# Weighting of the gathered expert rows moved between the first-layer banks of the recurrence's network; its last quarter finished in two halves

## The reference

```python
# s: a phase recurrence and a small network
context = jnp.concatenate([cm_real, cm_imag, ret_real, ret_imag], axis=-1)   # [B, S, 4*128]
h = _layernorm(context, ln_gamma, ln_beta)
h = jax.nn.gelu(jnp.einsum('bsd,ed->bse', h, W1) + b1, approximate=False)    # 256 wide: first layer
h = jnp.einsum('bsd,ed->bse', h, W2) + b2                                    # 128 wide: second layer
s = x + h
# g: experts with a capacity; each token's two gates weight the two rows it gets back
out = jnp.einsum('EGCM,GSEC->GSM', expert_outputs, combine)
x = x + s * silu(out)
```

## Time and profile before

| | |
|---|---|
| median of 3 runs | 681.86 us (681.68 to 682.83) |
| profiled execution, kernel time | 679.72 us |
| its span, first to last instruction | 677.8 us |
| TensorE busy | 598.5 us, 88% |
| VectorE busy | 483.6 us, 71% |
| ScalarE busy | 329.5 us, 49% |
| mean granted TensorE clock | 0.949 of full speed |

### The profile page before, as it was taken

One profiled execution on the slowest core, in us unless ns is written; L12 is line 12 of the kernel. 1 busy time (PEld: TensorE's weight loads), 2 busy tenths in 40 slices (PEclk: granted clock), 3 DMA queues, 4 the chain that ended last, 5 costly groups with the idle time before them and its releaser, 6 DMA issues.

```text
span 677.8 us, 12462 instructions
## 1 busy us (share of the span) xinstructions
PE 598.5 (88%) x4233; PEld 368.6 (54%) x4260; DVE 483.6 (71%) x1184; ACT 329.5 (49%) x586; POOL 159.6 (24%) x146
## 2 busy tenths in 40 slices
PE   2878999999999998999999958844999799999995
PEld 1524543534444446999999524342346356656553
DVE  7799989999888986555555882067998399832437
ACT  1742566665757666555555577520233352352322
POOL 2000000000233330333333100000078668722200
PEclk9877999999999999999999998966899799999997
DMA  8970606051631621111110510260012133310401
GB/s 187 253 268 3 226 2 196 17 181 45 173 96 33 167 83 38 48 49 50 47 47 25 154 43 1 57 195 0 0 43 64 21 104 107 99 37 16 120 20 62
DMA packets 53676, 57.18 MB, mean 84 GB/s; under 512 B 8635, under 2 KB 37339, under 8 KB 53579
## 3 DMA queue, kind: packets, MB, share of 16 engines
q1 hardware_dynamic: 49294, 49.73, 26.2%
q0 software_dynamic: 4320, 6.81, 3.1%
q10 hardware_dynamic: 12, 0.01, 0.0%
HBM read 42.19 MB, written 18.85 MB: 90 GB/s over the span
## 4 chain that ended last, share of the span: by engine, by line
PE 61%; DVE 26%; issue 5%; ACT 4%; DMA 1%; SPq 1%; another core or an unknown queue 0%; DVEq 0%; ACTq 0%
PE banks L1479 10%; PE banks L1600 7%; PE banks L1725 6%; PE banks L1541 6%; PE banks L1491 5%; PE banks L1558 5%; DVE arena L1071 5%; PE banks L1714 4%; DVE mpart L1074 4%; PE banks L1711 4%; PE banks L1770 3%; DVE mpart L1069 2%; ACT arena L693 2%; PE banks L1544 2%; PE banks L1423 1%
## 5 line engine op out<-in xcount | busy, mean ns | idle before, releaser
L693 ACT ACTIVATE arena<-banks 128x512 f32<-128x512 f32 (+1 forms) x304 | 156.1, 586 | 98.0 <-PE banks L1544 55.9
L1558 PE MATMUL banks<-arena 96*128 96x512 bf16 (+3 forms) x384 | 120.4, 344 | 6.6 <-DVE mpart L1071 2.0
L1541 PE MATMUL banks<-arena 128*128 128x512 bf16 (+3 forms) x358 | 106.7, 327 | 12.6 <-ACT arena L693 9.0
L1074 DVE TENSOR_REDUCE mpart<-banks 128x1 f32<-128x512 f32 x128 | 85.9, 684 | 9.5 <-PE banks L1558 9.0
L1071 DVE CUSTOM_DVE_ANT_0 arena<-banks,arena 128x512 bf16<-128x512 f32 (+1 forms) x128 | 76.7, 617 | 9.7 <-PE banks L1558 6.5
L1479 PE MATMUL banks<-arena 128*128 128x128 f32 x624 | 76.3, 275 | 1.0 <-ACT arena L643 1.0
L1479 PEld LDWEIGHTS banks<-arena 128*128 128x128 f32 x624 | 72.8, 192 | 1.5 <-ACT arena L643 1.5
L1600 PE MATMUL banks<-arena 128*9 128x512 f32 (+3 forms) x768 | 71.4, 491 | 0.0
L1541 PEld LDWEIGHTS banks<-arena 128*128 128x128 bf16 x384 | 37.6, 99 | 60.5 <-issue 27.3
L739 ACT ACTIVATE arena<-banks 125x512 f32<-125x512 f32 (+2 forms) x48 | 28.6, 596 | 78.7 <-PE banks L1711 55.3
L544 POOL DMA_INDIRECT slots<-rows_a,posn x16 | 15.5, 969 | 192.9 <-PE banks L1541 179.4
(11 more groups left out here) (268 smaller groups left out, 904.3 us busy)
## 6 DMA issues: line engine op xcount, KB each, us to landing
k_parts<-arena SPq DMA_DIRECT2D x6, 768.0 KB, 7.9
arena<-in_L_ffn_experts_w_dram SPq DMA_DIRECT2D x2, 2048.0 KB, 10.7
arena<-results SPq DMA_DIRECT2D x8, 512.0 KB, 6.8
arena<-k_parts SPq DMA_DIRECT2D x7, 576.0 KB
arena<-q_parts SPq DMA_DIRECT2D x28, 144.0 KB
arena<-in_L_ffn_w_kernel_dram SPq DMA_DIRECT2D x8, 344.0 KB
slots<-in_pad_rows_dram SPq DMA_DIRECT2D x1, 2535.0 KB, 11.8
arena<-slots SPq DMA_DIRECT2D x39, 65.0 KB
```

The costliest lines, as they stand in the source:

```text
L693: act.activation(Pr[:, r % 4, heads[0]:heads[-1] + 1, 0:n], ring_e[e % 3][:, 0:len(heads) * n].rearrange("p (j c) -> p j c", j=len(heads)) ...
L1074: ins = dve.tensor_reduce(part, ps[:, 0:n], AX_X, ALU.max)
L1541: ins = pe.matmul(ring_e[e % 3][:, at * n:at * n + n], QK[:, slot, j, 1, P * kt:P * kt + P], QK[:, slot, j, 0, q:q + n], start=True, stop= ...
L1558: ins = pe.matmul(ps[:, at * n:at * n + n], QK[0:TALL, slot, j, 0, P * i:P * i + P], QK[0:TALL, slot, j, 1, 512 * half:512 * half + n], st ...
```

## The change

VectorE's order is written anew: `weighted(0)` stands behind scaled(3), `weighted(1)` behind scaled(4), `finish(1, 0)` and `finish(1, 1)` behind scaled(6), and `finish(1, 2)` behind attended(2). The last quarter is finished by a new function, `last_half(i)`, in two halves of two tiles: three instructions of 256 columns each. For that, `layer_2(3)` puts its tiles 2 and 3 into the other bank of `psM`, signals after two tiles and again after four, and waits between them for attended(2), which reads that bank. SyncE stores the last quarter in two transfers.

```diff
-            for c in range(4):
-                sp.wait_ge(Z["x2_done"], c + 1)
-                sp.dma_start(out_t[:, 4 * c:4 * c + 4, :], x1[:, 4 * c:4 * c + 4, :]).then_inc(Z["out_done"], 16)
-            sp.wait_ge(Z["out_done"], 64)
+            for i, (t0, t1) in enumerate(((0, 4), (4, 8), (8, 12), (12, 14), (14, 16))):
+                sp.wait_ge(Z["x2_done"], i + 1)
+                sp.dma_start(out_t[:, t0:t1, :], x1[:, t0:t1, :]).then_inc(Z["out_done"], 16)
+            sp.wait_ge(Z["out_done"], 16 * 5)
...
-            for c in range(4):
-                scaled(2 * c)
-                scaled(2 * c + 1)
-                if c:
-                    attended(c - 1)
-                if c == 2:
-                    weighted(0)
-                    weighted(1)
-            for c in range(3):
+            def last_half(i):
+
+                tiles = slice(12 + 2 * i, 14 + 2 * i)
+                dve.wait_ge(Z["h2_ps"], 4 + i)
+                link(dve.tensor_tensor(s_sb[:, tiles, :], psM[:, 1 - i, 256 * i:256 * i + 256].rearrange("p (n d) -> p n d", d=D),
+                                       s_sb[:, tiles, :], ALU.add))
+                link(dve.tensor_tensor(ya[:, tiles, :], ya[:, tiles, :], s_sb[:, tiles, :], ALU.mult))
+                dve.tensor_tensor(x1[:, tiles, :], x1[:, tiles, :], ya[:, tiles, :], ALU.add).then_inc(Z["x2_done"], 1)
+
+            for u in range(4):
+                scaled(u)
+            weighted(0)
+            attended(0)
+            scaled(4)
+            weighted(1)
+            scaled(5)
+            attended(1)
+            scaled(6)
+            for c in range(2):
                 finish(1, c).then_inc(Z["x2_done"], 1)
-            attended(3)
-            finish(1, 3).then_inc(Z["x2_done"], 1)
+            scaled(7)
+            attended(2)
+            finish(1, 2).then_inc(Z["x2_done"], 1)
+            for i in range(2):
+                last_half(i)
...
-                        ins = pe.matmul(psM[:, c % 2, P * n:P * n + P], h1g[:, o, q:q + P], W2T_sb[:, o, :], start=(o == 0), stop=(o == 1))
-                ins.then_inc(Z["h2_ps"], 1)
+                        ins = pe.matmul(psM[:, (c + (c == 3 and n >= 2)) % 2, P * n:P * n + P], h1g[:, o, q:q + P], W2T_sb[:, o, :], start=(o == 0), stop=(o == 1))
+                    if n == 3 or (c, n) == (3, 1):
+                        ins.then_inc(Z["h2_ps"], 1)
+                    if (c, n) == (3, 1):
+                        pe.wait_ge(Z["s1_done"], 3)
```

## The result

| | before | after |
|---|---|---|
| median | 682.13 us (681.68 to 682.83, 5 runs) | 678.54 us (677.77 to 679.24, 5 runs) |
| ratio | | 0.9951, 95% interval 0.9938 to 0.9963 |
| profiled execution | 679.72 us, span 677.8 | 678.54 us, span 676.6 |

The change makes the kernel faster by 3.59 us between the medians, 2.5 to 4.2 by the interval. The forecast was 677.7, in a range from 676.2 to 679.8, with 0.93 on faster.

A forecast was written before the change was run, and what follows sets the result against it. Work on VectorE and ScalarE unrelated to the matmuls was taken to hold 11 us of the end; moved weighting and halves end VectorE at 671.35, plus 2.3 store: span 673.65, 4.15 less, median 677.7 us, range 676.2 to 679.8.

The forecast's parts named there:

- signs of being wrong: TensorE idle ahead of the last bank, DMA-ended idle ahead of line 1381, or the first 647 us changed.
- The moved weighting: VectorE: weighted(0) fits behind scaled(3), 4.25 us of work in 4.6; weighted(1) behind scaled(4) delays scaled(5) by 0.85 us.
- The closing of TensorE's hole: TensorE ahead of layer_2(3): it starts at 666.66 without a hole, 3.0 us earlier than before.
- The halves: VectorE's last quarter: six instructions at 0.416 us, ending at 671.35; the halving pays its own cost and no more.
- The store: Output's end: the span ends 2.3 us behind VectorE's last instruction instead of 2.77; bounds 2.77 and 2.27.
- The table loads: ScalarE around the two Silus: 1.28 us for each load, with the Gelu table back at 663.3.
- rival 1: ScalarE or TensorE still holds the end; TensorE idles again and returns at half clock: 679.1 us, chance 0.09.
- The thin spare: Ahead of layer_2(3): the Gelu of u=7 ends at 666.4, 0.3 us before layer_2(2) ends at 666.66.
- Rival 3: VectorE: weighted(0) waits for the expert rows in front of scaled(4); slower, 684 if they land at 656; chance 0.03.
- free up to 1.3 us: Rival 3's late expert rows: no cost up to some 1.3 us (Silu 660.9 against use at 662.2), then one for one.
- break-even at 5.5: Rival 3's expert rows: lateness decides against the change when they land 5.5 us after 648.3, at 653.8.

The follow-up runs named there:

- the weights first: SyncE issues expert 4's loads ahead of its wait for the scattered destinations: 669.66 us in the changed kernel, 673.95 us in the kernel before.
- the filler: Changed kernel with three or six chained multiplications of 128x1024 on a dead region ahead of weighted(0): 679.65 us with three, 683.92 us with six.

## Why the prediction was right

**The start of the stage.** One of my signs of being wrong did come: the first 647 us are not those of before, for scaled(3) starts at 650.60. It says nothing against the working from there on. The runs with the weights first, the old order and the new, start it at 641.93 and 642.10, so nothing shows that the change moves anything ahead of it, and 2.4 of the 3.0 us are the difference between two holes upstream.

**The moved weighting.** Right in place and size. With the 3.0 us of later start taken off, weighted(1) ends into a scaled(5) at 657.0 (said: 657.1), the first Silu starts at 659.8 (said: 659.8), the Gelu table is back at 663.1 (said: 663.3), scaled(7) starts at 664.9 (said: 664.95), VectorE ends at 671.34 (said: 671.35). Every term was a duration of a row and every start the later of two rows.

**What gains.** I put the gain to the moved weighting. The number came out because the sum had the finishes in their new place; the sentence named the wrong part. The weighting moved by itself is worth 0.2 to 0.3 us; it is the finishes of the first two quarters ahead of the end of layer_2(2) that shorten the end, by 2.6 us, and the weighting had to move only so far that the first Silu is done when finish(1, 0) could start. One weighting was enough for that. The closing of TensorE's hole, which I counted among the steps, gains little without the finishes. Finishes ahead with neither weighting moved was not run: they would wait for the Silus.

**The halves.** Right: 26.00 us to the end of the span with and without them. The six instructions took 0.42 to 0.43 us each, the nearest row had 0.416. The Trainium skill's figure (VectorE: DVE Perf Modes, the section on the TRN2 errata) of 424 ns, an estimate from the page's formula, agrees, and so does its warning: the halving buys nothing here in the new order.

**The store.** Right: 2.26 against 2.3, half of the transfer's 1.0 us.

**The table loads.** The Trainium skill (ScalarE: Activation LUTs, What ACT_TABLE_LOAD costs) counts 2.66 us for each change of tables, a load of 1283 ns and about 1380 ns to drain. The trace has the load at 664.79, 1.28 long, and the Gelu at 666.08, so the measurement has no such drain. As an estimate from the page's figure, two changes at 2.66 would have brought the Gelu of u=7 to its end near 670.2, and TensorE a hole of 0.5 us ahead of layer_2(3); there is none. In rival 1 I had said that a Gelu followed at once on both loads; in the rows it did on the second only, and the Silu behind the first waited 3.41 us for VectorE. In the profile after, both are followed at once.

**The thin spare and rival 1.** The Gelu of u=7 ended at 669.35, layer_2(2) at 669.67: 0.3 us, as said. That it lay so close did no harm, and would have done none: with only the first weighting moved, TensorE idles 0.40 us there, and the stage is the same. Nor did it return at half clock, as rival 1 has it: behind holes of 0.40, 0.77 and 1.70 us the last group took 2.05 us each time, at a clock of 1.00.

**Rival 3's terms.** Mis-sized. I put lateness as free up to 1.3 us and break-even at 5.5. In the changed kernel VectorE idles 0.46, 0.34, 2.80 and 1.09 us behind scaled(3), 4.69 in all (three of them in the rows shown, the 0.34 ahead of attended(1)), and every one of these can take up lateness; I had counted the slack of the first Silu alone. With the filler what is left idle is 1.83 us (three), ahead of the first finish, and 0.82 and 1.04 (six), ahead of scaled(6) and the first finish. So 2.86 and 2.83 us are taken up, and the rest is paid: 0.89 and 4.7 by this account, 0.79 and 4.71 measured. Break-even, as an estimate, is at 2.86 plus the gain of 3.6 to 4.2, between 6.4 and 7 us; with 7.5 us the kernel was slower than before.

**The 0.8 us between 677.7 and 678.54.** Of these, 0.27 us is the median of before itself (681.86 with three runs, 682.13 with five). The other 0.56 are the gain: the working took 4.15 off, the place gave 4.20 against the same profile, and the medians 3.59. There are two candidates for this 0.56. The last group of the old order takes 2.5 to 3.1 us, so that its stage varies from 26.8 to 27.4, and the old profile had the slowest; against the profile with 26.8 the gain is 3.57 us, that of the medians. And the wait for expert 4's weights, 6.9 to 7.9 us in the profiles of the changed kernel and seven variants, moves each execution as a whole. With that wait gone the medians differ by 4.1 to 4.3. Which of the two stages is the usual one, single profiles can't show, and it stays open.

## What to carry to other kernels

An engine that runs in order should get its independent work in the holes that already wait on the bound engine; find them by the idle time in brackets, and give each hole its price and its deadline. Then ask not which hole of TensorE closes but how much the in-order engine has left behind TensorE's last result: moving 2.7 us of finishes ahead of it was worth 2.6 us, closing a hole of 3 us alone 0.2 to 0.3. Splitting the last piece paid nothing here where its consumer, VectorE, was the bound: it cost there what the shorter last store gave back. And compare two profiles first by where the stage in question begins: here the spans differed by 1.2 us, the stage by 4.2, and a load queued behind an unrelated wait, 100 us earlier, cost twice what the whole change gained (682.32 to 673.95).

## What the hardware showed that I had not expected

- The same hole of 3.05 us in TensorE gave last groups of 2.53, 2.73 and 3.14 us: the granted clock was still 1.00 when the work resumed each time and fell to 0.50 (1.2 GHz) only inside the group, at another point in each execution. Behind holes of 0.40, 0.77 and 1.70 us it stayed at 1.00 for the whole group, and behind those of 4.26 and 6.86 us it was 0.50 from the first matmul on.
- Two Silus of 128x1024 back to back take 2.00 us together, where each alone takes 1.06.
- In the profile of before TensorE stands still for 4.26 us up to 535.62, and ScalarE for longer, with no releaser that the trace can name; the profile of the changed kernel shows no such stop there. It remains unexplained.
